# Two transformer layers on one core: first maxima in pairs, a wait moved off VectorE, the last group's head order, and wide masks added by VectorE

## The reference

```python
# layer 0: 32 heads of 16, one shared key/value head, no mask
Q = (x @ Wq + bq).reshape(B, N, H, d_h);  K = x @ Wk + bk;  V = x @ Wv + bv
attn = softmax(einsum('bnhd,bkd->bhnk', Q, K) * scale)
out = einsum('bhnk,bkd->bnhd', attn, V).reshape(B, N, D) @ Wo + bo
h = silu(gate) * up;  ffn = h @ w_down.T                 # inner width 1376
# layer 1: 32 heads of 16, 8 key/value heads, rotary positions, causal mask
scores = where(tril, einsum('bhqk,bkd...', xq, xk) / 4, -inf)
out = einsum('bhqk,bkhd->bqhd', softmax(scores), xv) @ Wo
ffn = x @ W_base.T + b_base + sum over 2 of 8 experts of a rank-16 product
```

## Time and profile before

| what | value |
|---|---|
| median of 3 runs | 1993.01 us (1991.43 to 1997.32) |
| profiled execution | 2006.2 us, span 2004.5 us |
| mean granted TensorE clock | 0.976 |
| PE busy / weight loads | 1914.6 us (96%) / 975.3 us (49%) |
| DVE / ACT / POOL busy | 1379.2 (69%) / 1088.6 (54%) / 232.4 us (12%) |
| shares of the chain that ended last | PE 81%, ACT 7%, DVE 4%, SP queue 4%, issue 2%, DMA 2% |

### The profile page before, as it was taken

How to read it: one execution, slowest core, us unless ns; L and a number is a source line. 1 busy time by engine, 2 the same in 40 slices (tenths; PEclk the granted TensorE clock), 3 DMA queues, 4 the chain that set the end, 5 groups by cost and what they waited for, 6 DMA issues and landing times.

```text
span 2004.5 us, 28840 instructions
## 1 busy us (share of the span) xinstructions
PE 1914.6 (96%) x10864; PEld 975.3 (49%) x10864; DVE 1379.2 (69%) x1719; ACT 1088.6 (54%) x2177; POOL 232.4 (12%) x606
## 2 busy tenths in 40 slices
PE   6999999999999999999999999999999999999998
PEld 5888887733333333333334335744543333333436
DVE  6554544425899999999996763756787777777733
ACT  4221212122787878878775774312257777677662
POOL 1000000000000000100000100000023433333330
PEclk9999999988999999999997899999999999999999
DMA  6010100043112211112212000103312212212102
GB/s 211 1 48 0 44 1 1 10 122 90 30 32 69 49 32 31 34 31 44 44 31 54 7 8 6 54 16 83 90 33 52 47 32 52 45 35 52 30 10 87
DMA packets 79211, 87.52 MB, mean 44 GB/s; under 512 B 19072, under 2 KB 52864, under 8 KB 79072
## 3 DMA queue, kind: packets, MB, share of 16 engines
q1 hardware_dynamic: 79072, 85.67, 17.2%
HBM read 55.20 MB, written 20.71 MB: 38 GB/s over the span
## 4 chain that ended last, share of the span: by engine, by line
PE 81%; ACT 7%; DVE 4%; SPq 4%; issue 2%; DMA 2%; POOL 0%; DVEq 0%; POOLq 0%; ACTq 0%; PEldq 0%
PE ps L1498 19%; PE ps L1528 11%; PE ps L1179 8%; PE ps L1180 7%; PE ps L1181 7%; PE ps L1435 7%; ACT arena L806 6%; PE ps L1524 6%; PE ps L1356 5%; PE ps L1362 4%; PE ps L1273 3%; SPq L468 2%; SPq L466 1%; DMA slots<-arena 1%; DVE arena L1043 1%
## 5 line engine op out<-in xcount | busy, mean ns | idle before, releaser
L806 ACT ACTIVATE arena<-ps 128x512 f32<-128x512 f32 (+3 forms) x1792 | 867.7, 556 | 325.5 <-PE ps L1528 171.4
L1043 DVE TENSOR_REDUCE arena<-ps 128x1 f32<-128x1024 f32 (+3 forms) x768 | 856.1, 1153 | 181.0 <-PE ps L1362 104.8
L1498 PE MATMUL ps<-arena 128*17 128x512 f32 (+3 forms) x3584 | 439.2, 562 | 1.0 <-ACT arena L806 0.6
L1362 PE MATMUL ps<-slots 48*128 48x512 f32 x1024 | 409.7, 474 | 8.8 <-DMA slots<-kparts 4.6
L1528 PE MATMUL ps<-slots 50*128 50x512 f32 x1024 | 387.9, 459 | 24.0 <-ACT arena L806 14.7
L1528 PEld LDWEIGHTS ps<-slots 50*128 50x128 f32 x1024 | 172.7, 188 | 326.7 <-ACT arena L806 269.1
L1524 PE MATMUL ps<-slots 98*128 98x512 bf16 (+3 forms) x768 | 207.7, 328 | 9.2 <-DMA slots<-arena 5.8
L1356 PE MATMUL ps<-slots 96*128 96x512 bf16 (+3 forms) x768 | 193.6, 328 | 13.8 <-DVE arena L1046 7.7
L1362 PEld LDWEIGHTS ps<-slots 48*128 48x128 f32 x1024 | 171.8, 190 | 66.7 <-DVE arena L1043 22.9
L606 POOL TENSOR_SCALAR_AFFINE_SELECT arena<-arena 128x128 f32<-128x128 f32 x512 | 145.3, 295 | 320.3 <-ACT arena L806 312.4
L667 ACT ACTIVATE xn<-ps 128x512 f32<-128x512 f32 (+1 forms) x44 | 26.3, 598 | 259.1 <-PE ps L1181 259.1
(11 more groups left out here) (127 smaller groups left out, 1855.3 us busy)
## 6 DMA issues: line engine op xcount, KB each, us to landing
slots<-qparts SPq DMA_DIRECT2D x96, 128.0 KB, 3.6
qparts<-arena SPq DMA_DIRECT2D x32, 256.0 KB
xnT<-arena SPq DMA_DIRECT2D x256, 32.0 KB
slots<-qparts SPq DMA_DIRECT2D x96, 64.0 KB, 3.3
qparts<-arena SPq DMA_DIRECT2D x48, 128.0 KB
slots<-qparts SPq DMA_DIRECT2D x32, 192.0 KB, 3.7
w_raw<-in_wgu SPq DMA_DIRECT2D x20, 256.0 KB, 3.2
acc<-in_x SPq DMA_DIRECT2D x4, 1024.0 KB, 8.0
```

The source lines that it names most:

```text
L806: act.activation(prob[local % P_RING][:, q0:CH], bank(local % SP_RING)[:, q0:CH], ACT.Exp, scale=SCALE).then_inc(S["p_ready"], 1)
L1043: dve.tensor_reduce(maxes[c][:, h[0] * TPC + qt:h[0] * TPC + qt + 1], src[:, 0:w], AX_X, ALU.max).then_inc(S["x_done"], 1)
L1362: last = pe.matmul(dst[:, k0:k1], q_slot[u][r:r + ROWS[0], c, h % 2, qt * P:(qt + 1) * P].bitcast(F32R), k_slot[u][r:r + ROWS[0], k0:k1].b ...
L1498: mm = pe.matmul(bank(7)[32 * h:32 * h + DH + 1, q0:CH], v_slot[n % SLOTS][:, kt, :], prob[idx % P_RING][:, q0:CH], start=(kt == 0), stop= ...
```

## The change

1. **First maxima of layer 0.** FIRST_MAX_AT goes from 12 to 13; the items now stand in pairs behind the parts k = 1 and k = 3, so four to a product instead of three. The matmuls of a pair are sorted by their key half: first half of both heads, then second half of both (the two heads lie in different row halves). lower(i - 1) moves from k = 0 to k = 1, behind that part's pair, and SyncE's copy of the first maxima row from i = 18 to i = 17.
2. **Maxima rows.** VectorE no longer waits for its own m_ready before it raises x_done; TensorE waits for m_ready where it reuses that item's banks, and at three other places.
3. **Last group of layer 0.** main_items gives the heads of the last group in the order 0, 2, 1, 3.
4. **Wide masks.** In layer 1, for c = 1, TensorE's mask product is left out, and VectorE's maximum becomes one tensor_tensor_reduce: scores (PSUM, float32) plus a mask (bfloat16, the last w columns of a 1024-column tile that is zero but for its last 128), maximum into one column, with the sum written to w_q, which is not used any more then. For c = 0 all stays.

```diff
-FIRST_MAX_AT = 12
-ROWS_AT = [18, 20]
+FIRST_MAX_AT = 13
+ROWS_AT = [17, 20]
...
+    heads = (0, 2, 1, 3) if n == GROUPS - 1 and not causal else range(HG)
+    return [(kt, h, max(0, kt - TPC * qc) * P if causal else 0) for kt in range(kts) for h in heads]
...
-    j = 3 * (i - FIRST_MAX_AT) + k
-    return range(j, j + 1) if i >= FIRST_MAX_AT and k < 3 and j < count else range(0)
+    j = 4 * (i - FIRST_MAX_AT) + k - 1
+    return range(j, min(j + 2, count)) if i >= FIRST_MAX_AT and k % 2 else range(0)
...
+def masked_by_vector(causal, c):
+    return causal and c > 0
...
-                    dve.wait_ge(S["m_ready"], n * QC + c + 1)
                     dve.sem_inc(S["x_done"], 1)
...
+                    if masked_by_vector(l == 1, c):
+                        masked = w_q[:, 2 * (j % 2):2 * (j % 2) + 2, :].rearrange("p k f -> p (k f)")
+                        dve.tensor_tensor_reduce(out=masked[:, 0:w], in0=src[:, 0:w], in1=mask_qk[:, N - w:N], scale=1.0, scalar=LOWEST,
+                                                 op0=ALU.add, op1=ALU.max,
+                                                 accum_out=maxes[c][:, h[0] * TPC + qt:h[0] * TPC + qt + 1]).then_inc(S["x_done"], 1)
+                        return
...
-                            if k == 0 and i:
+                            if k == 1 and i:
                                 lower(i - 1)
...
                         pe.wait_ge(S["x_done"], j if (n, c, qt) == (GROUPS - 1, 1, None) else j - 1)
+                        m, mc, mqt, _ = all_items[j - 2]
+                        if m is not None and mqt is None:
+                            pe.wait_ge(S["m_ready"], m * QC + mc + 1)
...
-                                         start=True, stop=k1 < w)
-                        if k1 == w:
-                            last = pe.matmul(dst[:, w - P:w], identb[:, :], mask_qk[:, :], start=False, stop=True)
+                                         start=True, stop=k1 < w or masked_by_vector(causal, c))
+                        if k1 == w and not masked_by_vector(causal, c):
+                            last = pe.matmul(dst[:, w - P:w], identb[:, :], mask_qk[:, N - P:N], start=False, stop=True)
...
+                    todo = [piece for piece in first if piece[0] in items]
+                    if not causal:
+                        todo.sort(key=lambda piece: piece[5])
```

More of the change, by code:

```diff
@@ L65, in width_f, with main_items @@
     return min(P, F - j * P)
-def main_items(causal, qc):
+def main_items(causal, qc, n=0):
     kts = TPC * (qc + 1) if causal else KT
-    return [(kt, h, max(0, kt - TPC * qc) * P if causal else 0) for kt in range(kts) for h in range(HG)]
+    heads = (0, 2, 1, 3) if n == GROUPS - 1 and not causal else range(HG)
+    return [(kt, h, max(0, kt - TPC * qc) * P if causal else 0) for kt in range(kts) for h in heads]
 def weight_views(t, j):
@@ L801, in attend @@
                         for c in range(QC):
[L802 removed]
+                            for i, (kt, h, q0) in enumerate(main_items(l == 1, c, n)):
                                 act.wait_ge(S["s_ready"], local + 1)
@@ L1040, in maximum @@
                     if qt is not None:
[L1041 to L1048, removed]
+                        reduce_maximum(src, n, c, qt, h, j)
                         return
@@ L1328, in tail_step @@
                         pe.wait_ge(S["x_done"], items_in_all)
+                        pe.wait_ge(S["m_ready"], GROUPS * QC)
                     last = passes(dst, xo_hi[:, c % 2, k, q], xo_lo[:, c % 2, k, q], wo_hi[:, k, :], wo_lo[:, k, :], k == 0, k == KC - 1)
@@ L1336, in _ @@
                 blocks = max_blocks(l == 1)
-                items_in_all = sum(len(b) for b in blocks)
+                all_items = [item for b in blocks for item in b]
+                items_in_all = len(all_items)
                 starts = [sum(len(b) for b in blocks[:n]) for n in range(GROUPS)]
@@ L1345, in max_piece @@
                         pe.wait_ge(S["x_done"], j - 1)
+                        pe.wait_ge(S["m_ready"], (GROUPS - 3) * QC + 2)
                         broadcast([dst[:, 0:CH], dst[:, CH:2 * CH]], c, h).then_inc(S["x_ready"], 1)
@@ L1443, in first_maxima @@
                 def first_maxima(items):
-                    for piece in first:
-                        if piece[0] in items:
-                            if piece[0] == 0 and piece[-2]:
-                                pe.wait_ge(S["slot_in"][0], 16 * 12)
-                                pe.wait_ge(*((S["b_evac"], TT) if l else (S["y_evac"], TT * len(ROUNDS) + 1)))
-                            max_piece(*piece)
+                    todo = [piece for piece in first if piece[0] in items]
+                    if not causal:
+                        todo.sort(key=lambda piece: piece[5])
+                    for piece in todo:
+                        if piece[0] == 0 and piece[-2]:
+                            pe.wait_ge(S["slot_in"][0], 16 * 12)
+                            pe.wait_ge(*((S["b_evac"], TT) if l else (S["y_evac"], TT * len(ROUNDS) + 1)))
+                        max_piece(*piece)
                 if l == 0:
@@ L1515, in attend @@
                         for c in range(QC):
-                            nkt = len(items[c]) // HG
-                            for i, (kt, h, q0) in enumerate(items[c]):
+                            items = main_items(causal, c, n)
+                            nkt = len(items) // HG
+                            for i, (kt, h, q0) in enumerate(items):
                                 if i == 0:
```

26 lines of the change are left out of this document (17 added, 9 removed).

## The result

| | before | changed |
|---|---|---|
| median of 4 runs | 1994.9 us (1991.43 to 1997.32) | 1968.86 us (1963.99 to 1972.42) |
| ratio, 95% interval | | 0.9858, 0.9814 to 0.9902 |
| profiled execution, span | 2006.2, 2004.5 us | 1963.99, 1962.3 us |
| mean granted clock | 0.976 | 0.990 |

What follows compares the result with a forecast made beforehand. TensorE was taken to bound the projections at half clock and layer 1's c = 1, ScalarE's chain layer 0's attention. 19.4 + 2.5 + 0 + 12.6 = 34.5 us off the median 1993.0 gave 1959, range 1946 to 1978.

Steps and rivals of the forecast that it cites:

- the first two rivals: No slow clock in the timed runs' projections (1970 us), and masks' time not kept (1971 us); chance 0.12 each.
- First maxima: Layer 0's projections: no long wait or halved clock, pairs every 3.0 us, products end at 476.5 instead of 495.9; 19.4 us.
- the first follows a pause that every execution has: Layer 0's projections: the timed runs were taken to have this low-clock stretch too, which costs 11 us.
- No pause behind a row: Maxima rows: TensorE resumes 0.05 us after m_ready, saving 0.06 us at each of some 46 rows; 2.5 us.
- Heads in turn: Layer 0's last group: two scores can start together, but the fourth still waits for the first exponential; nothing, within 3 us.
- Wide masks: Layer 1, c = 1: TensorE saves 0.06 us for each of 14 masks in 15 groups; 12.6 us.
- what it saves in c = 1 is kept: Layer 1's attention: c = 1 is bound by TensorE, busy for 19.27 of 19.50 us, so its savings there count.
- The second long stretch: Low clock in layer 0's attention, 1073.1 to 1114.1 us, costing 16 or so; the timed runs were assumed to lack it.
- The timed runs never had the slow clock in the projections: Rival: the first maxima are then worth 8.5 us and the time is 1970; chance 0.12.
- the masks' time isn't kept: Rival, layer 1's c = 1: VectorE's new instruction or exponentials become what a quad waits for; 1971 us, chance 0.12.
- The slower case: Rival: VectorE's new instruction at half rate, adding 0.88 us to each, c = 1 at 26.5 us; 2076 us, chance 0.07.
- the upper end: Layer 1, c = 1: VectorE's new instruction needs another 0.28 us for the maximum, costing some 5 us in all.

Runs made afterwards that it cites:

- first maxima alone: The kernel before with only the first maxima part (pairs from product 13, lowering behind part 1, row's copy at 17): 1978.09 us, ratio 0.9931.
- pairs from 12: The changed kernel with the pairs of first maxima starting at product 12, where the kernel before starts them: 1971.51 us, ratio 0.9869.
- early masks: The changed kernel with TensorE's mask product put back at four maxima, three of them in the first intervals of c = 1: 1974.01 us in one execution.
- rows ahead of the output: The changed kernel with layer 1's c = 1 maxima rows copied by SyncE ahead of the eight output transfers: 1955.47 us, ratio 0.9801 to the kernel before.

## Why the prediction was right, and where not

The direction held, and so did the mechanisms of the two large parts; that of the second part didn't. The gain was 26 to 28 us where the sum gave 34.5. The measured 1968.86 us lies 10 us above the forecast of 1959 and just outside the forecast's own range (1949 to 1968). It lies inside the range given (1946 to 1978), and nearer to the times of the first two rivals (1970 and 1971) than to the forecast. That the number is this close owes something to luck as well: it was set against the kernel before as a mixture of executions whose low clock isn't the same.

**First maxima, 19.4 us: right in the trace, too large for the runs.** Attention starts 20.3 us earlier; the slot's landing, 2.95 us for a pair (taken 3.0), the end of the products (475.6, forecast 476.5) and the 2.8 us behind them came as worked out. TensorE arrives 0.8 us earlier than forecast, so 1.17 us of the wait stay rather than 0.3, without harm. This execution was 0.74 us ahead already: its last products to k and v (w_kv) before the maxima start at 421.61, those of the kernel before at 422.35. The step that failed is that "the first follows a pause that every execution has", and so costs the same in every run: the pause hardly varies (4.6 to 4.8 us, 4.0 with pairs), the low clock behind it does (23.9, 23.9, 13.7, with pairs 3.4 us). That this is why the runs gave less than the profile is inferred, since no profile shows the timed runs. Timed alone the part gives 13.8 us, between the 8.5 of the full clock and the 20.3 of the profile, and in this profile the longer low clock behind attention's start, which isn't the part's, took 3.2 us of it back.

**No pause behind a row, 2.5 us: nothing.** The step was "the way from m_ready directly at 0.05 us". Measured, it is 0.15 us from the end of VectorE's instruction to TensorE's matmul; the wait on VectorE that was removed was already part of the 0.11. (The sum was off too: 46 x 0.06 is 2.8, not 2.5.) VectorE itself does go on earlier, but the earlier trace rows say that it has time to spare there.

**Heads in turn, 0: 0.2 us**, hidden by the wait for the first exponential, as said.

**Wide masks, 12.6 us: 9.7.** 0.06 us for a mask was right (0.057), and so was the duration taken for the new instruction. The step that failed is that "what it saves in c = 1 is kept": a c = 1 was taken as bound by TensorE as a whole, because it is busy for 19.27 of 19.50 us. Its first interval ends on the row and its second on ScalarE; the four masks there are worth 0.07 instead of 0.24. The two in c = 0 went into the transfer's wait, as forecast: it grew from 0.40 to 0.49 in the groups shown, from 0.35 to 0.41 where it is shortest, and c = 0 stayed at 10.57.

By these sizes the sum is 13.8 + 0 + 0.2 + 9.7 = 23.7 us, and the whole change gave 26 to 28. The difference is within what the runs leave open.

**The second long stretch.** I assumed that the timed runs "lacked the second". It is neither rule nor exception: group 13 took 65.6 to 72.3 us in five of the thirteen profiled executions (before, first maxima alone, pairs from 12, early masks, rows ahead of the output), 58.2 in one and 55.3 to 55.4 in seven, with and without each part of the change. So 17 of the 42 us between the two profiles are not the change's. The price of it, "16 or so", was about right (72.25 - 55.31 = 16.9); by the prediction's own terms, 41 - 18 - 5, it would be 18.

**The rivals.** "The timed runs never had the slow clock in the projections" came nearest in time, but its condition isn't met: all three profiles that have the first maxima as before show the slow clock, for 13.7 to 23.9 us. Of "the masks' time isn't kept" a little under a quarter came true (2.9 us of 12.6), by its second reason, the exponentials, and by the row, not by VectorE. The slower case fell with 1224 ns.

On the new instruction as two, which the upper end stood on: the Trainium skill, VectorE: DVE Perf Modes, section on two Vector instructions with no wait between them, counts such an operation as a main one and an accumulator read, and the trace agrees: 240 reads of the accumulator, 82 ns each, where my upper end had 0.28 us. They start together with the next instruction, and leaving them out changed nothing. The halving of which the Trainium skill, Vector Engine (DVE) Microarchitecture Reference, section on points that are easy to get wrong, speaks for two non-bf16 SBUF sources was judged not to apply. The new instruction doesn't have two such sources; with one in PSUM and one in bf16 it took 1224 ns against the reduction's 1222. Of two such sources this case shows nothing.

## What to carry to other kernels

An engine that is busy for 99% of a stretch need not bound every quad of it: before you count a removed instruction at its full spacing, look at the intervals between the starts of the work that sets the pace, and count those that lie in intervals which end on another engine at nothing. Fill a pause of TensorE with work that is there anyway; here the pause cost its own length plus a low clock whose length differed from run to run, so size such a gain by several executions or give both ends. And when two profiles are subtracted, take out first what other executions show, present or absent, whatever the change.

## What the runs showed of the hardware that was not expected

- The low clock (1.2 GHz) at a pause of 4.0 to 4.8 us lasted 3.4, 13.7, 23.9 and 23.9 us in four executions: three of work that is the same up to there and behind it, the shortest with pairs behind the pause; behind attention's start, with waits of 1.39 and 0.94 us, it lasted 6.8, 10.2 or 17.1 us. In group 13, where all thirteen do nearly the same work, six executions had 13.7 to 41.0 us of it and seven none.
- VectorE's tensor_tensor_reduce from PSUM plus a bfloat16 tile runs at the rate of the plain reduction (1224 ns for 1024 columns, 811 for 640), and its accumulator's read, 82 ns, is hidden under the next instruction.
- From the end of a VectorE instruction to a matmul that waits for its semaphore directly it was 0.15 us; by way of a VectorE wait on its own write and a second semaphore, 0.11. The detour was no slower than the direct way.
